# Attention and feed-forward block: the output projection moved from behind the first to behind the second feed-forward layer, side sums in the input buffer, next input loaded later

## The reference, cut to what matters

```python
xn = layernorm(x)
q, k, v = split(xn @ Wq + bq), split(xn @ Wk + bk), split(xn @ Wv + bv)   # 16 heads of 16
weights = softmax(rope(q) @ rope(k).T / sqrt(256))
attn = (weights @ v).reshape(b, n, 256) @ Wo + bo                         # the projection
h = relu(s0 * [xn, -xn] @ sign(k0)) * 2                                   # 512 -> 1024, FIRST
h = relu(s1 * h @ sign(k1)) * 2                                           # 1024 -> 1024, SECOND
ffn = s2 * h @ sign(k2)                                                   # 1024 -> 256, THIRD
return x + attn + ffn
```

## Time and profile before

| what | value |
|---|---|
| median of 3 runs | 2842.97 us (2841.0 to 2846.34) |
| profiled execution, its own time | 2845.93 us |
| its span in the profile | 2844.1 us |
| PE busy | 2647.0 us, 93% |
| ACT busy | 2095.7 us, 74% |
| DVE busy | 1092.7 us, 38% |
| POOL busy | 378.0 us, 13% |

### The profile page before, as it was taken

One profiled execution on the slowest core, in us unless ns is written; L12 is line 12 of the kernel. 1 busy time (PEld: TensorE's weight loads), 2 busy tenths in 40 slices (PEclk: granted clock), 3 DMA queues, 4 the chain that ended last, 5 costly groups with the idle time before them and its releaser, 6 DMA issues.

```text
span 2844.1 us, 49497 instructions
## 1 busy us (share of the span) xinstructions
PE 2647.0 (93%) x20423; PEld 1337.2 (47%) x20423; DVE 1092.7 (38%) x1689; ACT 2095.7 (74%) x2301; POOL 378.0 (13%) x309
## 2 busy tenths in 40 slices
PE   6787299999999999999999999999999999999997
PEld 3443144544454445454545444454455454444444
DVE  7999532323332324232322333232423223232322
ACT  4445278888888787887878687878878787878783
POOL 5888400000000000000000000000000000000000
PEclk9889699999999999999999999999999999999998
DMA  6666521222121212121212222121312122222213
GB/s 198 191 196 194 155 54 50 57 50 57 50 57 49 63 45 74 48 68 51 56 57 55 72 57 68 47 67 48 81 48 57 56 55 62 57 72 55 65 39 100
DMA packets 279701, 211.74 MB, mean 74 GB/s; under 512 B 183616, under 2 KB 227392, under 8 KB 272960
## 3 DMA queue, kind: packets, MB, share of 16 engines
q1 hardware_dynamic: 271040, 200.30, 25.8%
q10 hardware_dynamic: 8448, 8.39, 0.9%
HBM read 132.08 MB, written 76.55 MB: 73 GB/s over the span
## 4 chain that ended last, share of the span: by engine, by line
PE 80%; DMA 4%; DVE 2%; issue 1%; SPq 1%; POOL 1%; ACT 0%; POOLq 0%; DVEq 0%
PE ps_o L911 32%; PE ps_f L946 24%; PE ps_s L896 21%; DMA y<-rest_sum_d 3%; PE ps_f L959 2%; DMA heads_t<-heads 1%; POOL heads L1020 1%; DVE h_lo L1077 1%; DVE h_hi L1075 1%; PE ps_f L1001 0%; DMA q_rows<-row_shift 0%; DVE sums L1041 0%; SPq L797 0%; DMA probs<-rest_sum_d 0%; SPq L813 0%
## 5 line engine op out<-in xcount | busy, mean ns | idle before, releaser
L876 ACT ACTIVATE probs<-ps_s 128x1024 f32<-128x1024 f32 x2048 | 1935.5, 1034 | 533.5 <-PE ps_s L896 531.3
L911 PE MATMUL ps_o<-probs,v_ones 128*32 128x512 f32 x8192 | 1011.2, 600 | 0.0
L896 PE MATMUL ps_s<-q_rows,k_rows 50*128 50x512 f32 x4096 | 853.0, 437 | 33.5 <-DMA q_rows<-row_shift 32.7
L896 PEld LDWEIGHTS ps_s<-q_rows,k_rows 50*128 50x128 f32 x4096 | 366.5, 184 | 698.0 <-ACT probs L876 605.9
L1075 DVE TENSOR_SCALAR h_hi<-ps_f 128x512 fp32r<-128x512 f32 x224 | 154.4, 689 | 973.8 <-PE ps_f L946 973.7
L946 PE MATMUL ps_f<-h_hi,ffn_w 64*128 64x512 f32 x2048 | 406.1, 393 | 0.0
L946 PE MATMUL ps_f<-h_lo,ffn_w 64*128 64x512 f32 x2048 | 405.1, 391 | 0.0
L911 PEld LDWEIGHTS ps_o<-probs,v_ones 128*32 128x32 f32 x8192 | 200.6, 108 | 417.4 <-issue 321.8
L1020 POOL TENSOR_TENSOR heads<-heads,sums 128x512 f32<-128x512 f32 x64 | 82.5, 1289 | 2213.3 <-DVE sums L1041 2213.3
L1041 DVE RECIPROCAL sums<-sums 128x128 f32<-128x128 f32 x256 | 229.0, 926 | 1.7
L946 PEld LDWEIGHTS ps_f<-h_lo,ffn_w 64*128 64x128 f32 x2048 | 194.9, 186 | 37.9
(11 more groups left out here) (95 smaller groups left out, 1524.1 us busy)
## 6 DMA issues: line engine op xcount, KB each, us to landing
k_rows<-k_parts SPq DMA_DIRECT2D x128, 256.0 KB
q_rows<-q_parts SPq DMA_DIRECT2D x384, 64.0 KB
q_parts<-parts SPq DMA_DIRECT2D x32, 512.0 KB, 3.7
k_parts<-parts SPq DMA_DIRECT2D x32, 512.0 KB, 4.5
k_rows<-k_parts SPq DMA_DIRECT2D x128, 128.0 KB
x_chunk<-in_x ACTq DMA_DIRECT2D x16, 512.0 KB, 4.0
xn_t<-xnT SPq DMA_DIRECT2D x16, 512.0 KB, 4.5
v_heads<-v_sb SPq DMA_DIRECT2D x16, 512.0 KB, 5.2
```

What stands on the lines that cost most here:

```text
L876: nc.scalar.activation(probs[:, s % PBUF, half * 2 * C:(half + 1) * 2 * C], ps_s[:, half].rearrange("p c n -> p (c n)"), ACT.Exp, scale=SC ...
L896: last = nc.tensor.matmul(ps_s[:, half, w], k_rows[rows, u, t * P:(t + 1) * P], q_rows[rows, u, half], start=True, stop=True)
L911: last = nc.tensor.matmul(ps_o[32 * c:32 * c + 2 * DH], v_ones[:, u, t], probs[:, s % PBUF, c * C:(c + 1) * C], start=(t == 0), stop=(t == ...
```

## The change

The projection moves from round 6 (head 0) to round 31 (head 3), behind the last phase of SECOND. SECOND gets 45 visits for the same 128 parts and THIRD 15 for its 64, so that SECOND ends in round 30. The banks are numbered anew. SECOND's side sum moves from `headsT[:, 0]` to `xT[:, 1]`, since `headsT` now holds the heads until late; the load of the next `xT` therefore waits for the takes of SECOND, in SP's turn j = 2, and its split follows at step 57. In SP's turns the store of a head now comes before the load of `xT` and the store of `y`.

```diff
-SPLIT_AT = 44
+SPLIT_AT = 57
-PROJECT_AT = 6
 BURSTS = (2, 1, 2, 2, 1) * 2
+PROJECT_AT = 3 * len(BURSTS) + 1
...
-    counts = [[1, 2] * (FT // 2), [6] * FT, [3] * TT]
+    counts = [[1, 2] * (FT // 2), [6] * 5 + [5] * 3, [4, 4, 4, 3]]
...
 def place(projects, layer, phase):
-    if layer == FIRST:
-        return phase
-    return (FT + 1) * layer + phase + (TT if projects else 0)
-PROJECT_PLACE = FT + 1
+    return (FT + 1) * layer + phase + (TT if projects and layer == THIRD else 0)
+PROJECT_PLACE = 2 * (FT + 1)
...
-        carry = (xT[:, 0], headsT[:, 0])
+        carry = (xT[:, 0], xT[:, 1])
...
                         load_v(HEADS * i + (j + 2), u)
-                    if j == 1 and not last:
+                    if j >= 1:
+                        store_head(i, j - 1)
+                    if j == 2 and not last:
                         sp.wait_ge(xT_split, i + 1)
-                        sp.wait_ge(group_used, outs_before(i, projects) + place(projects, FIRST, FT) + 1 + BANKS)
+                        sp.wait_ge(group_used, outs_before(i, projects) + place(projects, SECOND, FT) + 1 + BANKS)
...
                         sp.dma_start(y_out[b - 1, r], y[:]).then_inc(y_stored, 16)
-                    if j >= 1:
-                        store_head(i, j - 1)
```

## The result

The changed kernel takes 2798.66 us (median of 4 runs, 2798.24 to 2802.49), the one before beside it 2841.98 (2840.68 to 2846.34). The ratio is 0.9848, 95% interval 0.9831 to 0.9865: 43.3 us less.

What follows compares the result with a forecast made beforehand. PE, in a ring with ACT, was taken as the bound, plus DMA waits and low clock at projections. Span 2844.1 - 70.2 + 21.9 = 2795.8, plus 1.8 gives 2797.6, lowered to 2796 us for a slow profiled execution; range 2784 to 2813.

Steps and rivals of the forecast that it cites:

- What bounds the kernel: PE busy 93%, in a ring with ACT; each of 12 projections costs 9.35 us, partly DMA waiting and low clock.
- Part 1: Projection in head 3: no DMA wait and no low clock, 3.5 us instead of 9.35 a pass.
- The sum: Whole kernel: span 2844.1 - 70.2 + 21.9 = 2795.8 us, with 1.8 around it 2797.6, taken as 2796.
- Part 2: SP's queue: xT's load moves behind a head's stores, landing at about 20.5 us into head 3; cost nothing.
- Part 3: SECOND in 45 visits: rounds 23, 25, 27, 28 and 30 get more parts, 1.39 us more a pass.
- Part 4: THIRD in 15 visits: five lighter rounds, of which one gains 0.02 us and the others nothing.
- Part 5: Side sum in xT instead of headsT: perhaps 0.4 us on DVE, inside 1.2 us of room; costs nothing.
- A: Rival: the denser rounds cost nothing, hidden by ACT or given back by THIRD; 2774 us; 8%.
- B: Rival: at the projection sum 2 or 3 waits for DVE, or it keeps its 5.85 us; 2820 us; 11%.
- C: Rival: xT lands over 15 us later than worked out, so PE pauses at 15 pass starts; 2892 us; 3%.
- D: Rival: PE's pause only moves, waiting elsewhere for ACT or a head's rows; 2868 us; 2%.
- The range: Whole kernel: 2784 to 2813 us, from the bounds on the projection's cost and on the visits' cost.

Runs made afterwards that it cites:

- the projection ahead of the `weigh`: Kernel with the projection moved but the old visits, its projection issued directly behind SECOND's last matmul, before round 32's `weigh`: 2793.31 us, ratio 0.9820.
- the visits alone: Kernel before with only SECOND in 45 visits and THIRD in 15, projection left in head 0: 2867.46 us, ratio 1.0087.
- the early loads: Kernel before, projection in head 0, with headsT and y loaded some 4 us earlier in 9 of 12 projecting passes: 2795.67 us, ratio 0.9837.
- side sum only: Kernel before with the side sum in xT, xT loaded in SP's turn j = 2 and split at step 57; projection and visits unchanged: 2843.59 us, ratio 1.0003.

## Why the prediction was right

The forecast was 2796 us, the result is 2798.66. By its steps:

- **What bounds the kernel.** A projection's 9.35 us were put down to 3.8 of waiting, 2.4 of low clock and 3.5 of work. With the wait taken away in place, a pass costs 149.17 - 145.70 = 3.5 us more than one without projection. Shown. The three add up to 9.7, a little more than the 9.35. The prediction gives all of that to ACT's catching up; some 0.1 of it is the last pass, if that was 1.3 us shorter before the change too.
- **Part 1, the wait goes.** Forecast 3.5 us for a projection at its new place. Measured 150.68 - 147.33 = 3.35 in the mean, and 150.78 - 147.33 = 3.45 without the last pass. Its terms, 3.48 + 0.15 - 0.15, were 3.65 - 0.19 in pass 5. Nothing was late in its stead: sum 2 had 1.2 us of room, and sum 3 0.9 where half a microsecond was forecast. That room is needed, as the projection ahead of the `weigh` shows. The sum's 70.2 us less were 12 x (9.35 - 3.35) = 72.0 in the profiles.
- **Part 2, the SP queue.** `xT` was forecast to be issued 16 us into head 3, to land at 20.5 and to be asked for at 24; it was issued at 13.9, landed at 18 and was asked for at 24.2. The store of a head is held in its stead, 11.34 us for four DMAs. How long `xT` itself was held before, which the prediction takes from the earlier trace rows, is not in that row but here:

```profile
L827 SPq DMA_DIRECT2D xT<-xn_t x15: 8192/9487/9985, 440.0 to 2582.6; - x15
```

Alone this part costs nothing (1.0003).
- **Part 3, SECOND denser.** Forecast 1.39 us a pass, rounds of 5.08, 5.08, 5.31, 5.31, 5.31; they were 5.08, 5.24, 5.29, 5.47, 5.29, together 1.67. The rule, the larger of ACT's time and PE's, held for three of five. What it missed is that in rounds 25 and 28 SECOND also changes its phase in mid-round, 0.16 us each; before, every change of SECOND lay at the start of a round. This is the term that was mis-sized most, 0.28 us a pass. With part 4 a pass costs 1.63 us instead of 1.37, so 16 x 0.26 = 4.2 us more than forecast. Part 1's 12 x 0.15 = 1.8 less take some of it back, which leaves 2.4; the result is 2.7 above. That the two errors go against each other is luck.
- **Part 4, THIRD gives nothing back.** Forecast 0.02 us a pass; it gave 0.05. With half of THIRD left out the time is still the same, so PE's side work is not the floor of these rounds. The prediction calls it ACT's; it is that of the ring, 3.77 us of ACT's work and 1.04 us of its waiting for PE.
- **Part 5, the side sum.** Nothing, and SECOND's take from `xT` is 0.69 us. The slower takes do not belong to the place: in the changed kernel FIRST's take from the same buffer lasts 1.10 us in pass 5, with POOL at work all through it, and 0.69 in pass 6, where POOL begins behind it.

```profile
1131.43 3.28 POOL L1014 TENSOR_TENSOR rest_sum<-rest_sum,bo 128x256 f32<-128x256 f32 x4 [5.37 <-DMA rest_sum<-in_x]
1131.63 1.10 DVE L1075 SCALAR_TENSOR_TENSOR h_lo<-xT,h_hi 128x512 fp32r<-128x512 f32 x1
...
1282.42 0.69 DVE L1075 SCALAR_TENSOR_TENSOR h_lo<-xT,h_hi 128x512 fp32r<-128x512 f32 x1
1283.62 1.44 POOL L1014 TENSOR_TENSOR rest_sum<-rest_sum,bo 128x256 f32<-128x256 f32 x2 [6.77 <-DMA rest_sum<-in_x]
```

Over the traces of both kernels 15 of the 48 takes from `xT` last 1.1 us or more, and all 15 have POOL at work through their whole length; the other 33 last 0.69, with POOL idle or beginning while they run. No run takes POOL's work away, so the cause is not shown.
- **The rivals.** A, that the denser rounds are hidden, fell with the visits alone (+26 us). B, a new wait at the projection, did not come at this place, but does where no `weigh` covers DVE's takes (+18 us). C, `xT` late, did not happen; forced, it costs a pause of 19.8 us at each of 15 pass starts. D, the pause moving elsewhere, fell with the result itself and with the early loads.
- **The range.** The bounds that it names, 0.3 us less to 1 more for each of 12 projections and a third of 21.9 either way, add up to 2785 and 2815, not 2784 and 2813. The result lies inside both.

The change thus holds two opposite parts: the move, worth 66 us (2841.65 to 2775.43), and the visits, which give back 23 of them (2798.66 - 2775.43). The visits make SECOND end two rounds earlier, which the projection does not need.

## What to carry to other kernels

Before moving work away from a wait, ask which load is late and by how much: here issuing two loads 4 to 5 us earlier in 9 of 12 passes brought as much as the whole change (2795.67 against 2798.66). In a ring of two engines that are nearly level, work added to some rounds costs its time, less the little room that the ring leaves (0.15 us behind a one-step round here), and work taken from others returns next to nothing, so an uneven deal of the same total is a loss. A pause of the matrix engine costs more than its length, since the work behind it may run at half clock.

## What the runs showed of the hardware

The clock did not fall with every pause of the same length: behind 3.08 us of waiting it fell, behind 2.97 it did not (passes 9 and 13 of the visits-only kernel). The length does not separate them: of the 39 waits at the projection in the four kernels that have them (before, visits only, side sum only, early loads), 2.8 to 4.8 us long, this is the only one whose matmuls took 3.72 us; behind all others, shorter ones too, they took 5.1 to 6.8. Without such waits the clock stood at 1.00 for the whole of passes 1 to 15 of the changed kernel. The start of a new phase in mid-round left a weight load idle for 0.29 to 0.32 us and made a round without room 0.16 us longer; what the weight load waits for stays open.
